# Wide attention: turnings from quad 5 on, behind half of the output product; decay attention: a front in another order

## The reference

```
# decay (16 heads of 8), x after a layer norm
qkv = (x @ w_qkv.T + b_qkv).reshape(B, T, 3, H, dh)
std_logits = einsum('bhqd,bhkd->bhqk', q, k) * scale
w1 = x_prev @ w1_write.T; w2 = x @ w2_write.T     # "write" lines, 4 numbers a head
r1 = x @ w1_read.T;       r2 = x @ w2_read.T      # "read" lines
write_lines, read_lines = exterior(w1, w2), exterior(r1, r2)   # 6 numbers, normalised
incidence = einsum('bqhp,bkhp->bhqk', read_lines, J_write)
weights = sigmoid(decay_logits) ** (q - k) where q > k, else 0
logits = std_logits + incidence * weights * bias_scale, -inf where k > q
out = softmax(logits) @ v @ w_out.T + b_out

# wide (16 heads of 64), x after a layer norm
q, k = _l2norm(q) * q_scale, _l2norm(k) * k_scale
attn = softmax(einsum('bhid,bhjd->bhij', q, k) * DH ** -0.5)
out = einsum('bhij,bhjd->bhid', attn, v) @ Wo + bo
```

## Time and profile before

| what | us |
|---|---|
| median of 3 runs (lowest to highest) | 5602.24 (5595.87 to 5605.1) |
| the profiled execution's own time | 5598.34 |
| its span, on which the rows' times count | 5596.5 |
| decay attention, front / from its first product on | 127.7 / 849.6 |
| wide attention, from its first load to its end | about 1770 |

### The profile page before, as it was taken

How to read it: one execution, slowest core, us unless ns; L and a number is a source line. 1 busy time by engine, 2 the same in 40 slices (tenths; PEclk the granted TensorE clock), 3 DMA queues, 4 the chain that set the end, 5 groups by cost and what they waited for, 6 DMA issues and landing times. The chain is left out here.

```text
span 5596.5 us, 97013 instructions
## 1 busy us (share of the span) xinstructions
PE 4584.3 (82%) x31060; PEld 2303.6 (41%) x31060; DVE 3680.8 (66%) x7243; ACT 3464.9 (62%) x5541; POOL 1407.4 (25%) x1422
## 2 busy tenths in 40 slices
PE   6999859568989976968888758699989989989758
PEld 2222359524444436932222245233333333333345
DVE  5443464477777776457777771777877777777671
ACT  5999745425555545547888723566767766766523
POOL 1101047524334305732233047000000000000037
PEclk8999979779999987979999878799999999999978
DMA  3222222213233322232223233100000000000133
GB/s 86 66 52 67 59 52 50 72 57 90 87 94 88 94 60 61 49 97 57 58 54 66 58 66 55 51 1 0 0 0 0 0 0 0 0 0 0 41 63 55
DMA packets 228307, 266.50 MB, mean 48 GB/s; under 512 B 36906, under 2 KB 194442, under 8 KB 221640
## 3 DMA queue, kind: packets, MB, share of 16 engines
q1 hardware_dynamic: 184468, 195.51, 13.1%
q0 software_dynamic: 43520, 66.97, 6.7%
HBM read 164.90 MB, written 96.65 MB: 47 GB/s over the span
## 5 line engine op out<-in xcount | busy, mean ns | idle before, releaser
L4037 ACT ACTIVATE prob_wide<-slot_wide,peak_wide 128x1024 f32<-128x1024 f32 x512 | 544.4, 1120 | 72.2 <-PE slot_wide L3898 70.8
L2184 ACT ACTIVATE prob_decay<-slot_decay 128x640 f32<-128x640 f32 x512 | 358.7, 705 | 342.2 <-PE slot_decay L2031 341.0
L1000 ACT ACTIVATE prob_rms<-slot_rms 128x1024 f32<-128x1024 f32 x512 | 504.1, 1092 | 56.2 <-PE slot_rms L834 53.8
L2518 DVE TENSOR_TENSOR slot_decay<-slot_decay,dtab_decay 128x512 f32<-128x512 f32 (+3 forms) x1024 | 454.0, 493 | 128.4 <-PE slot_decay L2010 108.4
L1000 ACT ACTIVATE prob_relative<-slot_relative 128x1024 f32<-128x1024 f32 x512 | 497.8, 1049 | 40.9 <-PE slot_relative L834 39.4
L1373 DVE TENSOR_TENSOR prob_relative<-prob_relative,rtab_relative 128x1024 f32<-128x1024 f32 (+1 forms) x256 | 394.9, 1548 | 134.8 <-ACT prob_relative L1000 126.6
L3913 PE MATMUL obank_wide<-prob_wide,v_wide 128*64 128x512 f32 x2048 | 467.7, 598 | 2.4 <-DVE zT_wide L4198 2.4
L3898 PE MATMUL slot_wide<-qT_wide,kT_wide 64*128 64x512 f16 x3072 | 401.3, 390 | 16.0 <-ACT prob_wide L4037 13.5
L4222 POOL TENSOR_TENSOR X<-X,bo_t_wide 128x512 f32 (+1 forms) x16 | 20.3, 1268 | 1562.6 <-DVE xn_wide L198 1542.3
L4184 DVE TENSOR_TENSOR sums_wide<-sums_wide,prob_wide 128x1024 f32<-128x1024 f32 x256 | 312.5, 1221 | 14.6 <-ACT prob_wide L4037 1.3
L858 PE MATMUL obank_relative<-prob_relative,vaug_relative 128*32 128x512 f32 x2048 | 275.8, 611 | 40.1 <-DVE prob_relative L1373 38.6
(11 more groups left out here) (893 smaller groups left out, 10382.6 us busy)
## 6 DMA issues: line engine op xcount, KB each, us to landing
scratch_decay<-parts_decay SPq DMA_DIRECT2D x192, 128.0 KB, 2.4
qst_decay<-scratch_decay SPq DMA_DIRECT2D x128, 128.0 KB
scratch_rms<-parts_rms SPq DMA_DIRECT2D x96, 128.0 KB
kst_rms<-scratch_rms POOLq DMA_DIRECT2D x96, 128.0 KB, 5.5
kst_decay<-scratch_decay SPq DMA_DIRECT2D x192, 64.0 KB
kin_decay<-scratch_decay SPq DMA_DIRECT2D x192, 64.0 KB
scratch_relative<-parts_relative SPq DMA_DIRECT2D x96, 128.0 KB
kst_relative<-scratch_relative POOLq DMA_DIRECT2D x96, 128.0 KB, 6.3
```

The lines of the kernel that those rows point to most:

```text
L1000: nc.scalar.activation(prob[:, Q % 2, p:G:2, at:at + m], slot[:, u % 3].rearrange("p (k c) -> p k c", k=2)[:, :, 0:m], ACT.Exp).then_inc(e ...
L2184: nc.scalar.activation(prob[:, Q % 2, j, 0:c1 - c0], slot[:, u % 3, c0:c1], ACT.Exp).then_inc(exp_done, 1)
L2518: last = nc.vector.tensor_tensor(sl, sl, dtab[:, h, 0:m], ALU.mult)
L4037: nc.scalar.activation(prob[:, Q % 2, u % 4, :], slot[:, u % 2, :], ACT.Exp, scale=peak[:, 1:2]).then_inc(exp_done, 1)
```

## The change

In the wide attention the steps of the next batch stand in other places. QK's halves stand at A and C of quads 1 to 4 (before: quads 1 to 3), NORM t at A of quads 2 to 5 (before: 1 C, 2 B, 3 B, 4 A), the eight TURNs from 5 B to 7 C (before: 4 B to 7 C), Y 0 at 5 A (before: 6 B). There is a new place M, between the third and the fourth score step, behind Z, which itself moves to between these two; it has one V and two of the TURNs.

```diff
-        HALVES_AT = {(1, "A"): (0, 0), (1, "B"): (0, 1), (1, "C"): (1, 0), (2, "A"): (1, 1), (2, "C"): (2, 0),
-                     (3, "A"): (2, 1), (3, "B"): (3, 0), (3, "C"): (3, 1)}
-        TURNS_AT = {(4, "B"): 0, (4, "C"): 1, (5, "A"): 2, (5, "C"): 3, (6, "A"): 4, (6, "C"): 5, (7, "A"): 6, (7, "C"): 7}
+        HALVES_AT = {(1, "A"): (0, 0), (1, "C"): (0, 1), (2, "A"): (1, 0), (2, "C"): (1, 1), (3, "A"): (2, 0),
+                     (3, "C"): (2, 1), (4, "A"): (3, 0), (4, "C"): (3, 1)}
+        TURNS_AT = {(5, "B"): 0, (5, "C"): 1, (6, "A"): 2, (6, "M"): 3, (6, "C"): 4, (7, "A"): 5, (7, "M"): 6, (7, "C"): 7}
...
                 yield "S", 4 * Q + 2
-                yield "S", 4 * Q + 3
                 if pv:
                     yield "Z", (Q - 1) % C
+                yield from bench_steps(Q, "M", prev, nxt)
+                yield "S", 4 * Q + 3
```

```diff
+                                keys = (qb + 1) * P
+                                for k in range(2):
+                                    nc.tensor.matmul(
+                                        slot[:, i % 3, k * S:k * S + keys],
+                                        qst[0:KR, 2 * m + k, qb * P:(qb + 1) * P], kst[0:KR, 2 * m + k, 0:keys],
+                                        start=True, stop=False, skip_group_check=True)
                                 for k in range(2):
                                     last = nc.tensor.matmul(
-                                        slot[:, i % 3, k * S:(k + 1) * S],
-                                        qst[0:KR, 2 * m + k, qb * P:(qb + 1) * P], kst[0:KR, 2 * m + k, :],
-                                        start=True, stop=True, skip_group_check=True)
+                                        slot[:, i % 3, k * S + keys - P:k * S + keys], negb[:], identb[:],
+                                        start=False, stop=True, skip_group_check=True)
...
-                            sp.dma_start(shifts.rearrange("j r t -> r j t"), gturn[:]).then_inc(guard_stored, 16)
-                            sp.wait_ge(guard_stored, 16)
-                            sp.dma_start(qst[KR:KS], shifts.rearrange("j (h b) t -> j h (b t)", h=H)
-                                         ).then_inc(guard_moved, 16)
+                            for j in range(3):
+                                sp.dma_start(qst[KR + j:KR + j + 1].rearrange("a h (b t) -> a (h b) t", t=P),
+                                             gturn[:, j, :]).then_inc(guard_moved, 16)
...
+                    if step == "MASK":
+                        dve.wait_ge(tab_act, 2 + 2 * H)
+                        own = dtab[:, :, 0:P]
+                        link(nc.vector.tensor_tensor(own, own, past[:, 0:P].unsqueeze(1).to_broadcast([P, H, P]),
+                                                     ALU.mult))
+                        dve.sem_inc(ready, 1)
```

More of the change, by code:

```diff
@@ L1564, in decay_attention @@
         READY = 4 if relative else 3
+        EARLY = 7 * TPB
         PLANS = {
@@ L1652, in schedule @@
             yield "GUARD",
+            if not prev:
+                yield "MASK",
             if decay:
@@ L1900, in do @@
                     o = b - 1
-                    if step == "START" and at_start(b, 0):
+                    if step == "MASK":
                         pe.wait_ge(ready, READY)
@@ L2109, in _ @@
                     nc.scalar.copy(lw[:], obank[:, 0:256]).then_inc(setup_act, 1)
-                    act.wait_ge(setup_dve, 3)
-                    for h in range(H):
-                        nc.scalar.activation(dtab[:, h, :], ahead, ACT.Exp, scale=lnd[:, 0, h:h + 1]
-                                             ).then_inc(tab_act, 1)
                 def do(b, step, *a):
@@ L2174, in do @@
                             act.wait_ge(tab_act, H)
+                        act.wait_ge(tab_act, 2 + H)
+                        for h in range(H):
+                            nc.scalar.activation(dtab[:, h, :], dtab[:, h, :], ACT.Copy, scale=bs_t[:, h:h + 1]
+                                                 ).then_inc(tab_act, 1)
                         act.sem_inc(ready, 1)
+                    if step == "TABLE":
+                        act.wait_ge(setup_dve, 3)
+                        for h in range(*a):
+                            nc.scalar.activation(dtab[:, h, :], ahead, ACT.Exp, scale=lnd[:, 0, h:h + 1]
+                                                 ).then_inc(tab_act, 1)
                     if step == "S":
@@ L2298, in _, with sums_of, spreads_of, roots_of @@
                     dve.sem_inc(setup_dve, 1)
+                def sums_of(tiles):
+                    for t in tiles:
+                        last = nc.vector.bn_stats(stats[:, t, 0:6], X[:, t, :])
+                    link(last)
+                def spreads_of(tiles):
+                    for t in tiles:
+                        last = nc.vector.bn_aggr(stats[:, t, 6:8], stats[:, t, 0:6])
+                    link(last)
+                def roots_of(st):
+                    link(nc.vector.tensor_scalar(st[:, :, 8], st[:, :, 7], 1e-5, None, ALU.add))
+                    rsqrt(nc, link, st[:, :, 9], st[:, :, 8], st[:, :, 10])
+                    dve.sem_inc(stats_ready, 1)
+                statistics(nc, link, X[:, 0:TPB], stats[:, 0:TPB], TPB)
+                dve.sem_inc(stats_ready, 1)
+                sums_of(range(TPB, EARLY))
                 dve.wait_ge(loaded, LOADED)
@@ L2317, in _ @@
                                             ALU.subtract).then_inc(setup_dve, 1)
-                def decay_table(heads):
-                    for h in heads:
-                        dve.wait_ge(tab_act, 3 + h)
-                        last = nc.vector.scalar_tensor_tensor(
-                            out=dtab[:, h, :], in0=dtab[:, h, :], scalar=bs_t[:, h:h + 1], in1=past,
-                            op0=ALU.mult, op1=ALU.mult)
-                    link(last)
+                link(nc.vector.tensor_copy(negb[:], negf))
+                link(nc.vector.tensor_copy(identb[:], ident[:]))
                 if relative:
@@ L3681, in bench_steps @@
                 yield "Y", 1
-            if Q == 6 and place == "B":
+            if Q == 5 and place == "A":
                 yield "Y", 0
```

56 lines of the change are left out of this document (17 added, 39 removed).

## The result

| | before | after |
|---|---|---|
| median of 5 runs, us | 5601.34 (5592.97 to 5605.1) | 5569.13 (5566.95 to 5572.57) |
| span of the profiled execution, us | 5596.5 | 5570.7 |
| decay front, first instruction to first bias product | 127.66 | 97.81 |
| decay stage, from batch 1's turning of the sizes to batch 15's | 748.3 | 766.8 |
| wide loop, 14 periods | 1486.46 | 1477.66 |

The ratio is 0.9948 (95% interval 0.9935 to 0.9961): 32 us faster where 101 were forecast, and outside the forecast's range. The front gave what it should, or nearly. The rest of the decay stage took 18.5 us of that back, and the wide loop gave 9 us where 67 were expected. (The stages ahead of the decay one, which the change leaves alone, were 3.6 us shorter in the profiled execution after than in the one before.

A forecast was written before the change was run, and what follows sets the result against it. The decay front was taken as bound by a chain of waits, the wide loop nearly by PE. From 5598.3 us, 67 (4.5 a period, 15 times) and 35 (front) gave 5496 profiled, 5500 as median; range 5458 to 5550.

The forecast's parts named there:

- The front: Decay attention from first instruction to first score product: 35 us shorter, bounds 27 and 41.
- DVE's chain: Wide loop, Y 1 to first turning: 47.4 us; PE loses 4.8 us instead of 8.6, gain 3.8 a period.
- Quads 6 and 7: Wide loop: second of two turnings around one score step waits 1.85 us for its bank; loss 2.2 a period.
- The clock: Wide loop, quad 4: the 4.58 us wait and its low clock go, gain 2.3 us a period.
- so I take none: Wide loop: no clock cost for the new 2.4 us wait, as full speed followed a 2.36 us wait before.
- Rival (2): Wide loop: clock falls at new waits; slower 4%, about equal 3%, only ahead of Y 0 (5534 to 5558) 12%.
- The longer guard: Decay batches: PE skips the guard in 15 batches, its code now twice as long; the sum took no cost.
- Rival (3): Decay stage: each skip of the longer guard costs PE 5.76 us, 86 us in all, end 5586; 4%.
- The guard starts: Decay front: the guard's start, now waiting for the stacks' transfers, comes 20.6 us earlier.
- Its loop: Decay front, guard's 32 steps: 26.2 us against 39.6, gain 13.4; between 23.8 and 28, low clock assumed.
- The rest gave 1.7 (1.2): Decay front's tail: one transfer instead of two in a row, 4.4 us against 5.6, gain 1.2.
- the statistics as free under the loads: Decay front: first batch's statistics run on DVE during the loads, xn ready at 1076.1; everything behind 8.65 us earlier.

The follow-up runs named there:

- front_only: The kernel before with the change to the decay attention alone, without the wide change: 5585.43 us, ratio 0.997.
- turn_b: The changed kernel with the second turning of quads 6 and 7 directly behind R (place B instead of M): 5519.5 us, ratio 0.9851.
- sum_late: turn_b plus the old, shorter guard code in batches 1 to 15, DVE's first sums of quads 4 and 5 moved behind Z3 and the fourth normalisation: 5462.96 us.
- wide_only: The kernel before with the change to the 64-wide attention alone, without the decay change: 5588.41 us, ratio 0.9975.
- z_late: The changed kernel, but DVE empties the middle turning of quads 6 and 7 ahead of Z instead of behind it: 5537.11 us, ratio 0.9887.

## Why the prediction failed, point by point

The prediction names the right waits and prices most of them within 0.3 us; it leaves out what two of them set off.

- *DVE's chain.* Right. 47.4 us from Y 1 to the first turning were forecast, 4158.97 - 4111.41 = 47.56 were measured. The wait ahead of Y 0 is 2.69 us (2.4), that ahead of the first turning 0.99 (0.7).
- *Quads 6 and 7.* Right: 1.80 and 1.89 us in place C (1.85), 0.70 at (6, A) (0.7).
- *The clock.* **This is the step that failed.** "so I take none" rested on one pair of waits in one execution. In the changed kernel's own last batch the same wait (2.35 us, 2.36 before) is followed by a PV of 5.35 us:

```profile
5226.23 5.35 PE L3923 MATMUL obank_wide<-prob_wide,v_wide 128*64 128x512 f32 x16 [2.35 <-DVE zT_wide L4208]
```

  The fall at quad 4 that was to be gained, 2.3 us, came back as 3.0 in quads 6 and 7. Rival (2) had the mechanism, but its likeliest form put it at Y 0 alone, and I gave it 19% in all its forms. A steady period is 105.85 us, 4.1 above the 101.7 forecast. 3.0 of it is clock and 0.2 the stretch up to the first turning, where the two longer waits (0.6) stand in place of smaller ones. The rest, about 1 us, is small pieces behind it, most of all that a turning for which PE waited takes 1.25 us from start to start and not 1.02.
- *The longer guard.* Rival (3) was right in kind, and its 4% was far too little. It expected 5.76 us at each of 15 jumps; three batches were about 5 us longer, some about 1, and the stage 18.5 in all. This is the second step that failed: the sum had put the term at nothing. That "the skips of today do not show it" was weak evidence, since the thing that the change doubles is what decides whether they do.
- *The front.* Forecast 35, measured 29.9, within the bounds of 27 and 41. The guard starts 1121.88 - 1060.09 = 61.8 us into the stage, 17.0 earlier (20.6). Its loop lasts 28.4 us to the end of the last reduction, 39.5 before, 11.2 less (13.4), with the clock low, as assumed. That is just above the forecast's upper end of 28, and part of it is a slip in the sum: eight masks of 128 columns were put at 0.96 us, but by the prediction's own row (0.457 us for 512 columns, 0.03 of it to start) they take 1.1 and the loop 27.8. The rest gave 1.7 (1.2).

The 3.6 us missing at the guard's start can be followed in the rows. The timeline of DVE, then of POOL, then of PE, at the stage's start:

```profile
1061.82 1.92 DVE L191 TENSOR_SCALAR stats_decay<-stats_decay 128x4 f32<-128x4 f32 x1
1063.77 3.54 DVE L165 TENSOR_SCALAR stats_decay<-stats_decay 128x4 int32<-128x4 int32 x1
1067.34 0.34 DVE L166 TENSOR_SCALAR stats_decay<-stats_decay 128x4 int32<-128x4 int32 x1
```
```profile
1060.20 3.51 POOL L2219 MEMSET vaug_decay<- 128x4096 f32 x1 [22.06 <-POOLq L2705]
1063.77 3.51 POOL L2220 MEMSET qst_decay<- 128x4096 f32 x1
```
```profile
1076.91 1.08 PE L1912 MATMUL bench_decay<-ident_decay,sq_decay 128*128 128x128 f32 x4 [4.38 <-ACT woT_decay L2114]
```

In the kernel before, where they stand later in the stage and no memset runs beside them, the same two operations on 128x4 elements take 0.17 us each; here they took 1.92 and 3.54, and each ended within 0.03 us of POOL's memset (1063.71, 1067.28). The traces of front_only, turn_b and sum_late repeat this (1.92 and 3.53). So the early statistics end 5.1 us late. Behind them stand 24 of the other tiles' sums (4.74 us), which the change put there, and only then the decay logits, for which ACT waits 3.53 us; PE in turn waits 4.38 us for ACT's copy of the output weights. The Trainium skill (SBUF — State Buffer, SBUF: two separate sides) says that GpSimd and some DVE instructions, those in a 2-port perf mode among them, share a pair of ports, which whichever starts first holds for its whole instruction; the ends of the rows agree, and the trace does not name the mode. I had counted the statistics as free under the loads. This is read from the rows; neither a kernel without the memsets beside them nor one with the 24 sums behind the logits was run.

As to the sum: the profiled execution should have been 102 us shorter and is 25.8. Of the 76 us that are missing, the loop has 58 (67 - 8.8), the jumped guard 18.5 and the front 5.1; 5.6 us came from elsewhere, 3.6 of them ahead of the decay stage.

Open is which waits of 1.8 to 2.7 us are followed by a low clock in a given kernel. The same wide code had three waits of 2.13, 1.96 and 1.95 us in its first period in wide_only, with full clock behind all of them; in the changed kernel they are 2.15, 1.96 and 1.95 us, and the clock falls behind the last two. No run here forecasts that; the runs only show that the loop without such waits, sum_late's, is free of it.

## What to carry to other kernels

Where a trace shows a fall of the clock behind any wait, price every wait of TensorE of a similar length (here from 1.8 us on) with a range: the wait alone, up to the wait plus the 1.4 to 2.3 us that the low clock took behind one here. Expect to get back less than that where another engine is close behind, and prefer an order that cuts one long wait into two short ones: the same moved sum was worth nothing where it only moved a wait, and 45 us, with its twin, where it brought all of them under 1.4. Longer code that is jumped over cost time here though it never ran; keep the fast form for the batch that runs it and a short form elsewhere (13 us here), and look at every engine that jumps. When two engines empty one bank, look up in a neighbouring place of the same schedule how the turn-over works there: quad 5 had the answer for quads 6 and 7.

## What the runs showed of the hardware

- The low clock behind equal waits alternates from period to period in one execution (z_late: 102.93 and 104.56 us, Y 0 at 3.83 or 5.46 us).
- Code that never runs cost time: 128, 256 and 384 jumped products and loads a batch on PE gave 748.3, 766.8 and 785.3 us for fourteen batches, with 171, 179 and 186 instruction packets on one queue, and PE stood with nothing to wait for. Without any jumped code, on DVE either, it was 736.6 us and 163 packets, and what went was waiting for DVE.
- A DVE instruction that takes 0.17 us elsewhere took 3.54 us beside a POOL memset, as shown above.
